# A graph network on one core: first layer's second product on full 128-row tiles, sender factors looked up with edges on partitions, one padding round of gathers left out

## What is computed

```python
h = relu(layernorm(x))
x = x + L0(h, src, dst)      # h scaled by out_degree**-0.5, summed over edges, times in_degree**-0.5
h = relu(layernorm(x))
# L1: encoders, then two steps over all edges and all nodes, then a decoder
n = ln(mlp(h));  e = ln(mlp(edge_attr))
for s in range(2):
    e = e + ln(mlp(concat(e, n[src], n[dst])))
    agg = segment_sum(e, dst)
    n = n + ln(mlp(concat(n, agg)))
out = x + mlp(n)
```

## Time and profile before

| | |
|---|---|
| median of 3 runs | 12197.94 us (12151.58 to 12213.49) |
| the profiled execution, its own time | 12234.22 us |
| its span, from first to last instruction | 12231.8 us |
| mean granted TensorE clock | 0.709 of full speed |
| busy: PE, PEld, DVE, ACT, POOL | 78%, 57%, 44%, 44%, 73% |

### The profile page before, as it was taken

The page is one execution under the profiler, slowest core; times in us unless marked ns, Lnnn a source line. Parts: engine busy times, 40 slices in busy tenths (PEclk is TensorE's granted clock), DMA queues, the critical chain, the costliest instruction groups (busy, mean ns, idle before and its releaser), DMA issues. The chain is left out here.

```text
span 12231.8 us, 206351 instructions
## 1 busy us (share of the span) xinstructions
PE 9512.5 (78%) x62224; PEld 6999.0 (57%) x62225; DVE 5436.7 (44%) x10951; ACT 5439.7 (44%) x8544; POOL 8971.4 (73%) x9433
## 2 busy tenths in 40 slices
PE   5889989999999967777777777776667677777776
PEld 4667777777788745555555555554444444444444
DVE  9744444455555534444444444443333333333333
ACT  0024444455555534444444444444444444444444
POOL 6757777777777367777777777776777777777776
PEclk8755555555555577777778777777777777777777
DMA  2222222222222233333333333342222222222222
GB/s 70 69 46 38 39 39 39 38 43 49 48 48 48 46 84 96 94 96 96 94 98 104 103 104 102 104 100 70 69 69 70 69 69 71 72 72 72 73 73 59
DMA packets 1311379, 869.26 MB, mean 71 GB/s; under 512 B 831441, under 2 KB 991442, under 8 KB 1309949
## 3 DMA queue, kind: packets, MB, share of 16 engines
q1 hardware_dynamic: 906914, 580.85, 16.9%
q0 software_dynamic: 301056, 231.81, 10.7%
q10 hardware_dynamic: 102736, 48.45, 1.5%
HBM read 629.10 MB, written 247.05 MB: 72 GB/s over the span
## 5 line engine op out<-in xcount | busy, mean ns | idle before, releaser
L1951 POOL DMA_INDIRECT edge_blk_g<-sender_part,idx_all x6272 | 5919.7, 944 | 2151.5 <-issue 1910.7
L148 POOL DMA_INDIRECT gather_ring<-sender_x,idx_all x2784 | 2631.8, 945 | 919.4 <-issue 843.2
L2007 PE MATMUL edge_blk_hps<-ident,edge_blk_g 128*128 128x128 f32 x6256 | 1224.6, 357 | 1971.1 <-DMA edge_blk_g<-sender_part,idx_all 1970.5
L2007 PEld LDWEIGHTS edge_blk_hps<-ident,edge_blk_g 128*128 128x128 f32 x6256 | 1048.5, 252 | 2723.7 <-DMA edge_blk_g<-sender_part,idx_all 2690.8
L2023 ACT ACT_TABLE_LOAD x1564 | 2006.6, 1283 | 59.3 <-ACTq L1113 31.5
L2095 DVE SCALAR_TENSOR_TENSOR agg<-edge_blk_aggps,vecs,agg 64x64 f32 x1564 | 441.9, 283 | 3073.7 <-PE edge_blk_aggps L1967 2919.0
L2037 ACT ACTIVATE edge_blk_h<-edge_blk_hps,vecs 128x512 f32<-128x512 f32 x782 | 537.2, 687 | 2794.7 <-PE edge_blk_hps L2007 2779.2
L2002 PE MATMUL edge_blk_hps<-edge_blk_oha,edge_blk_win 128*128 128x512 f32 x1564 | 1153.5, 828 | 27.8 <-DMA edge_blk_win<-receiver_part 27.8
L1990 PEld LDWEIGHTS edge_blk_yps<-w_edge_blk,edge_blk_h 64*128 64x128 f32 x12512 | 1011.0, 242 | 243.4 <-issue 243.4
L1990 PE MATMUL edge_blk_yps<-w_edge_blk,edge_blk_h 64*128 64x64 f32 x12512 | 1133.7, 336 | 0.0
L1656 ACT ACT_TABLE_LOAD x782 | 1003.3, 1283 | 274.1 <-PEq L91 260.3
(11 more groups left out here) (275 smaller groups left out, 12122.9 us busy)
## 6 DMA issues: line engine op xcount, KB each, us to landing
edge_blk_e<-edge_state SPq DMA_DIRECT2D x782, 256.0 KB
edge_blk_g<-sender_part,idx_all POOLq DMA_INDIRECT x6272
edge_state<-fl_e SPq DMA_DIRECT2D x391, 256.0 KB
edge_blk_dlb<-local_dst SPq DMA_DIRECT2D x1564, 64.0 KB
edge_state<-edge_blk_new SPq DMA_DIRECT2D x391, 256.0 KB
gather_ring<-sender_x,idx_all POOLq DMA_INDIRECT x2784
edge_blk_win<-receiver_part SPq DMA_DIRECT2D x1564, 16.0 KB
fl_attr<-attr_slots SPq DMA_DIRECT2D x391, 32.0 KB
```

What stands on the lines that cost most here:

```text
L148: pool.indirect_dma_start(out=gr[:, n % RING, j, :], out_offset=None, in_=table, in_offset=bass.IndirectOffsetOnAxis(ap=idx_all[:, 8 * n + ...
L1951: pool.indirect_dma_start(out=g[n % QUAD][:, i, 64 * c:64 * c + 64], out_offset=None, in_=ps_d, in_offset=bass.IndirectOffsetOnAxis(ap=idx ...
L2007: ins = nc.tensor.matmul(h_ps[n.half][:, P * i:P * i + P], g[n.b][:, i, :], ident[:, :], start=False, stop=i == TILES - 1)
```

## The change

- Lookup: the operands of `look` change places. The one-hot of 128 edges is now the stationary one, and the table's three parts of 128 columns stream past it: 24 matmuls a round in place of six of 512 columns. The result has edges on partitions. `pick` is then eight instructions of 128 columns that compare a row of numbers with each edge's low digit (`lo_e`, taken from `idx_all`), multiply, and write the sum out as well (`accum_out`). `total`, its column of ones, its PSUM banks, the spreading DMA of the low digits and the thirty dummy matmuls are gone.
- `EARLY` 44 to 40 and `AHEAD` 53 to 46.
- The float copy of each block's sender list moves from ACT to DVE.
- Setup: ACT's square root comes ahead of its wait for the copied lists.
- First layer: `second` is one bias matmul of 512 columns and four of 128 rows by 128 columns (the weights are block-diagonal), into one PSUM bank, the two banks taken by rounds in turn, so it waits for the norm of two rounds back. `encode` has weights of 128 rows, 64 of them zeros. The dummies of `stream` are gone.
- `every_round` issues rounds 0 to 390.

```diff
-EARLY = 44
-AHEAD = 53
+EARLY = 40
+AHEAD = 46
...
-    for n in range(first, FAST_ROUNDS):
+    for n in range(first, FAST_ROUNDS - 1):
         body(n)
...
+                    act.wait_ge(s_var, 1)
+                    nc.scalar.activation(rinv[:, :], red[:, :], ACT.Sqrt, bias=eps_c[:, 0:1], scale=1.0 / X_DIM).then_inc(s_dev, 1)
                     act.wait_ge(s_cp, 64)
...
-                    act.wait_ge(s_var, 1)
-                    nc.scalar.activation(rinv[:, :], red[:, :], ACT.Sqrt, bias=eps_c[:, 0:1], scale=1.0 / X_DIM).then_inc(s_dev, 1)
...
-                    nc.scalar.activation(srow_f[:, :], srow[:, :], ACT.Copy)
...
+                    if later(k):
+                        dve.wait_ge(tr_done, k)
+                    v.tensor_copy(srow_f[:, :], srow[:, :]).then_inc(srow_ok, 1)
...
                 def pick(r):
                     dve.wait_ge(z_ok, r + 1)
                     if r >= 2:
-                        dve.wait_ge(fac_ok, r - 1)
-                    v.scalar_tensor_tensor(picked[r % 2], lo_bc[r % 3][:, :], part_f[:, 0:1],
-                                           z_ps[r % 2][:, :, :].rearrange("p c e -> p (c e)"), ALU.is_equal, ALU.mult).then_inc(picked_ok, 1)
+                        dve.wait_ge(picked_ok, r - 1)
+                    for j in range(8):
+                        at = 8 * r + j
+                        ins = v.scalar_tensor_tensor(unsummed[:, r % 2, j, :], row_f[:, :], lo_e[:, at:at + 1],
+                                                     z_ps[r % 2][:, j // TILES, P * (j % TILES):P * (j % TILES) + P], ALU.is_equal, ALU.mult,
+                                                     accum_out=fac[:, at:at + 1])
+                    ins.then_inc(picked_ok, 1)
...
-                    for c in range(2):
+                    for j in range(8):
                         for i in range(3):
-                            ins = nc.tensor.matmul(z_ps[r % 2][:, c, :], r_parts[0:NHI, i, :], hi_hot[r % 2][0:NHI, CHUNK * c:CHUNK * c + CHUNK],
-                                                   start=i == 0, stop=i == 2)
+                            ins = nc.tensor.matmul(z_ps[r % 2][:, j // TILES, P * (j % TILES):P * (j % TILES) + P],
+                                                   hi_hot[r % 2][0:NHI, P * j:P * j + P], r_parts[0:NHI, i, :], start=i == 0, stop=i == 2)
...
-                for _ in range(30):
-                    nc.tensor.matmul(z_ps[1][:, 1, :], busy[:, 0:P], busy[:, :], start=True, stop=True)
                 pe.wait_ge(parts_ok, 1)
-                look(0)
                 for r in range(EARLY):
-                    if r + 1 < EARLY:
-                        look(r + 1)
-                    total(r)
+                    look(r)
...
-        attr_t = many(2, "attr_t", [64, P])
+        attr_t = many(2, "attr_t", [P, P])
...
-        y_ps = ctx.enter_context(nc.psum_tensor("fl_yps", [P, 2, 512], F32))
+        y_ps = [ps("yps0"), ps("yps1")]
...
-                    wait(pe, t_ok, n.back(1))
-                    for c in range(2):
-                        nc.tensor.matmul(y_ps[:, c, 0:TILES * D], one_bf[:, :], b1_parts[:, 0:TILES * D], start=True, stop=False)
+                    wait(pe, t_ok, n.back(2))
+                    y = y_ps[n.half]
+                    nc.tensor.matmul(y[:, :], one_bf[:, :], b1_parts[:, :], start=True, stop=False)
                     for i in range(TILES):
-                        for c in range(2):
-                            q = slice(64 * c, 64 * c + 64)
-                            ins = nc.tensor.matmul(y_ps[:, c, D * i:D * i + D], h[n.half][q, P * i:P * i + P], w_mid[q, q],
-                                                   start=False, stop=i == TILES - 1)
+                        ins = nc.tensor.matmul(y[:, P * i:P * i + P], h[n.half][:, P * i:P * i + P], w_mid[:, :],
+                                               start=False, stop=i == TILES - 1)
...
-                    if i is None and (n.b == QUAD - 1 if not isinstance(n.m, int) else n.n < 6):
-                        stream(8)
```

More of the change, by code:

```diff
@@ L138, in every_round @@
     with pool.If(sort > 0):
-        for n in range(FAST_ROUNDS, MAX_ROUNDS):
+        for n in range(FAST_ROUNDS - 1, MAX_ROUNDS - 1):
             body(n)
@@ L732, in edge_lists @@
         hi_bc = [sb(f"hi_bc{i}", [P, ROUND], BF16) for i in range(3)]
-        lo_bc = [sb(f"lo_bc{i}", [P, ROUND], BF16) for i in range(3)]
-        one_f = sb("one_f", [P, 1])
-        busy = sb("busy", [P, CHUNK], BF16)
+        lo_i, lo_e, fac = sb("lo_i", [P, EARLY * 8], I32), sb("lo_e", [P, EARLY * 8]), sb("fac", [P, EARLY * 8])
+        unsummed = sb("unsummed", [P, 2, 8, P], BF16)
         one_lo = [sb(f"one_lo{i}", [P, most_lo * P], BF16) for i in range(2)]
@@ L779, in rows @@
                     if later(k):
-                        for waited, value in ((rows_f, k), (digits, k)):
+                        for waited, value in ((rows_f, k), (srow_ok, k)):
                             sp.wait_ge(waited, value)
@@ L875, in _ @@
                 v.memset(zeros[:, :], 0.0).then_inc(zero_ok, 1)
-                v.memset(one_f[:, :], 1.0).then_inc(zero_ok, 1)
-                v.memset(busy[:, :], 1.0).then_inc(zero_ok, 1)
                 v.memset(deg[:, :], 0.0).then_inc(zero_ok, 1)
                 v.memset(zero_col[:, :], 0.0).then_inc(zero_ok, 1)
-                dve.wait_ge(zero_ok, 5)
+                dve.wait_ge(zero_ok, 3)
                 dve.wait_ge(base_in, 32)
@@ L974, in scale @@
                     rows = gr[:, first:last, :, :].rearrange("p r j c -> p (r j) c")
-                    v.tensor_tensor(rows, rows, fac_ps[k % 2][:, 0:8 * (last - first)].rearrange("p (r j) -> p r j", j=1).broadcast_to(
+                    v.tensor_tensor(rows, rows, fac[:, 8 * first:8 * last].rearrange("p (r j) -> p r j", j=1).broadcast_to(
                         [P, 8 * (last - first), X_DIM]), ALU.mult).then_inc(scaled, 1)
+                dve.wait_ge(lists_ok, LIST_BLOCKS)
+                v.tensor_scalar(lo_i[:, :], idx_all[:, 0:EARLY * 8], P - 1, None, ALU.bitwise_and).then_inc(lo_step, 1)
+                dve.wait_ge(lo_step, 1)
+                v.tensor_copy(lo_e[:, :], lo_i[:, :]).then_inc(lo_step, 1)
+                dve.wait_ge(lo_step, 2)
                 hot(0)
@@ L1613, in body @@
                         rest_of_weights(n)
-                def stream(k):
-                    for _ in range(k):
-                        nc.tensor.matmul(n_ps[:, :], one_bf[:, :], b1_parts[:, :], start=True, stop=True)
                 def rest_of_weights(n):
@@ L1635, in _ @@
                 pe.wait_ge(s_ld, weights_landed)
[L1636 removed]
+                nc.tensor.matmul(y_ps[0][:, 0:NVEC], mean_w[:, :], vecs[:, :], start=True, stop=True).then_inc(s_vm, 1)
                 pe.wait_ge(s_diag, 1)
                 k = VEC.index("edge_enc")
[L1639 removed]
+                nc.tensor.matmul(y_ps[1][:, 0:D], ones_d[:, :], diag[k][:, :], start=True, stop=True).then_inc(s_rows, 1)
                 pe.wait_ge(prepared, 1)
[L1641 removed]
                 last = rounds_and_nodes(pe, body, count_sb, 2)
@@ L1661, in scale @@
                     wait(act, y_ok, n)
-                    nc.scalar.activation(sq[:, :, :].rearrange("p (c i) d -> p c (i d)", c=2), y_all, ACT.Square).then_inc(sq_ok, 1)
+                    nc.scalar.activation(sq[:, :, :].rearrange("p k d -> p (k d)"), y_ps[n.half][:, :], ACT.Square).then_inc(sq_ok, 1)
                     wait(act, red_ok, n)
@@ L1827, in rest_of_weights @@
                         step(v.tensor_tensor(vecs[:, c:c + 1], vecs[:, c:c + 1], n_ps[:, m:m + 1], ALU.add))
+                for a in attr_t:
+                    step(v.memset(a[:, :], 0.0))
                 for b in range(QUAD):
@@ L1838, in _ @@
                 dve.wait_ge(s_vm, 1)
[L1839 removed]
+                step(v.tensor_copy(vmean[:, :], y_ps[0][:, 0:NVEC]))
                 centre_bias(["edge_enc"])
```

64 lines of the change are left out of this document (23 added, 41 removed).

## The result

| | before | after |
|---|---|---|
| median | 12203.60 us (4 runs, 12151.58 to 12213.49) | 11993.07 us (4 runs, 11992.40 to 11994.65) |
| profiled execution, its span | 12231.8 us | 11991.4 us |
| mean granted TensorE clock | 0.709 | 0.779 |

The ratio is 0.9836, with a 95% interval of 0.9808 to 0.9864. The runs of before are those of the table ahead and one more (12209.26); they spread over 0.5%, those of after over 0.02%.

A forecast was written before the change was run, and what follows sets the result against it. It took POOL's gathers to bound both edge steps and PE's loop the first layer. 12231.8 − 211 = 12021, with 2.4 around the span 12023, scaled by 0.3% to 11988 (chance 0.60); range 11935 to 12060.

The forecast's parts named there:

- The scaling: Whole time: profiled execution is 0.3% over the median of the runs, so the span sum of 12023 becomes 11988.
- Setup: Before the lists: ACT's root issued at once when the variance is ready, near 19.6 us; −4.4 us.
- Lists: Making of sender lists: float copies on DVE +4.5 us, fewer copies −1, low digits +0.8; all together 0, first look near 483.6.
- Lookup: Lookup rounds on DVE: eight picks of 0.36 us plus `hot` 0.48, 3.36 us a round (2.9 to 4.2), 40 rounds 134 us.
- POOL goes on at 628: End of the lookup: POOL resumes gathers at 628, not 738; its 46 rounds issued by 588, never the late one.
- First layer, POOL: First layer's gathers: 345 rounds at 9.99 us, 3448 us from 628 to 4076; smaller lead costs 60 us.
- First layer, PE: First layer's loop: 8.44 us a round, merge giving 0.1 to 0.15, through at 3937, before POOL's 4076; catches up near round 300.
- The rule against the merge: First layer's products: a weight load overlaps a running matmul only when row groups differ; halves had this, full tiles don't.
- padding round: End of edge steps: dropping it costed at nothing; rival that it was on the path, each step 10 us earlier, 11968, chance 0.05.
- Cold first layer: Rival, first layer: clock may stay at 0.5 without dummies and with other shapes, rounds of 8.86 us; 12006, chance 0.18.
- In series: Rival, lookup: hot, look and pick run one after the other, 6.2 us a round, 114 us of gain gone; 12102, chance 0.10.
- slower: Rival, first layer: full-row loads and streams don't overlap, 3.2 us more a round, 11.6; about 13090, chance 0.03.

## Why the prediction came out as it did

The forecast of 11988 lies 5 us below the median of 11993, and the mechanism (the first layer turns from PE's pace to POOL's) is the one that came. That it lies so near is luck, for two misses cancel in it: the sum gave a span of 12021, and 11991.4 came, while the scaling took 36 us off.

- **The scaling** of the profiled execution by 0.3%, 36 us, was a step that failed. Only kernels whose first layer ends with PE have such a spread: 0.35 to 0.95% in the groups of before, 0.37% with the lookup alone. Once POOL ends it, profiled execution and median agree within 0.03%. So the 36 us most likely lay in PE's first layer, which the change takes off the path, and nothing of them was left to scale; this is inferred from which kernels spread, as there is only one trace of before. The span's sum should have stood as it was, at 12023, and it would then have been 30 us over the median that came.
- **Setup:** −4.4 forecast. The first gather came 7.6 us earlier. I let ACT's table load stand behind the variance; with no wait ahead of it the load was done at 10.7. The variance came 1.6 us earlier too (16.1, not 17.7), and DVE's pause is 0.47 us.
- **Lists:** all together 0 forecast, first look near 483.6; `hot`, which comes just before it, starts at 475.74. The added copy on DVE cost nearly nothing: the lookup alone, without the setup's edit, has its first `hot` at 483.46, 0.7 later than before.
- **Lookup:** 3.36 us a round forecast (8 x 0.36 + 0.48). From the first pick at 479.13 to 591.7, less 5.8 us for three `scale`, 40 rounds take 107 us, 2.67 each. The picks are 0.27 apart, not 0.36: a record of 0.34 us starts 0.07 before the last one ends, which the two rows I drew the line through could not show, and the accumulator's read is hidden. It is two instructions, as the Trainium skill, "VectorE: DVE Perf Modes", section "Two Vector instructions with no wait between them", says, and the trace has 320 such reads; what they cost here is 0.014 us each at most.
- **POOL goes on at 628 forecast**, 598.21 came: 7.9 us from the earlier start, 26.6 from the shorter rounds, less 4.7, since the start came 8.16 us after POOL's own end and not 1.8 after DVE's. "Never the late one here" was wrong: POOL ended its 46 rounds at 590.05, with the lookup.
- **First layer, POOL:** 345 rounds, 3448 us forecast; from 598.21 to 4045.2 it took 3447. The next step came 45.4 us after that; 44.3 forecast.
- **First layer, PE:** 8.44 us a round and a catch-up near round 300 forecast; 6.9 us and round 160 came. The step that failed is that the clock stays. With the old shapes and no dummies the loop is 8.5 us, it catches up only after some 350 rounds, and the time is the same, so the miss changed nothing in the time. The prices of the pieces were right: 0.21 apart at the lower clock.
- **The rule against the merge**, of the Trainium skill, "TensorE: Matmul & The Clock Gate", Part 3, "The mechanism": at the lower clock the full pieces took 1.91 us for eight, the halves 1.97 for sixteen. So the pieces gave 0.06 us, and with the bias (0.40 us to the first piece, not 0.53) the merge gave 0.19 where 0.1 to 0.15 was forecast. What it gave beyond came from the clock, of which that section's rule says nothing. The prediction called 0.110 us a half piece and 0.214 a full one agreement with the rule. They are not: a half piece streams 64 columns and a full one 128, so both cost the same a column, and no price of a lost overlap shows in them.
- **Second bank, padding round, edge steps:** nothing forecast; 6.8 against 6.9 us a round without the bank, 1 us a step at most for the padding, 3951.5 us for the step.
- **The rivals.** Cold first layer: its condition holds in the kernel with the old shapes (clock 0.52 to 0.57), but its 12006 did not come (11993.87), since the round there is 8.5 us, which POOL hides, and with node work 8.8 and not 9.06 (91 transposes in 2600 to 3400). In series, no effect, and slower did not come: DVE was busy 95% of the lookup, and the full pieces came no more than 0.21 us apart. Nor did the steps end 10 us earlier without the padding round.

## What to carry to other kernels

When a stage goes from one engine's pace to another's, find that other engine's end first: here the dummies alone and the merge alone each brought the first layer to it (span 170 and 168 us less), the lookup alone gave 131, and all together 240. The 70 us beyond the dummies are all POOL's: its pause before the first layer falls from 71 to 8 us, and its first gather comes 7.6 earlier. New lookup and dropped dummies, with the old shapes, reach the same 11993.87. Do not scale a forecast by the spread of the kernel before, if the change takes away what spreads. Once an engine is the whole path, count its own rounds in every stage before believing that a wait elsewhere sets a start.

## What the runs showed of the hardware

- **The granted clock rose with the rows of the products, while PE was busy less.** In 1000 to 1400, the old shapes kept PE busy 367 of 400 us at 0.52, the new ones 264 of 400 at 0.91. Going from 64 to 128 rows in the encoder, with the new rows all zeros, raised it from 0.52 to 0.74 and, with the second product on 128 rows, from 0.56 to 0.91. Ones in one operand did the same. Dummies of 96 rows and 512 columns, eight in every fourth round, did not raise it (0.54 with, 0.53 without; 0.86 with, 0.91 without).
- **The same fp32 pieces cost nearly half at that clock:** 1.91 us for eight at the lower, 1.06 at the higher.
- **A gather is slower to issue while the lists are made.** POOL's group in the changed kernel in 240 to 340, and in 475 to 515:

```profile
L148 POOL DMA_INDIRECT gather_ring<-normed_x,idx_all x66 | 81.7, 1239 | 20.1 <-issue 20.1
...
L148 POOL DMA_INDIRECT gather_ring<-normed_x,idx_all x33 | 31.4, 951 | 10.1 <-issue 10.1
```

With its 0.30 us of issue one takes 1.54 us in the first stretch and 1.25 in the second, with the same table and ring. What differs is the other engines' work and the transfers for the lists. With POOL the whole path, that is the next place to look: some 280 gathers by 476 us at 0.29 us more each are 80 us, an estimate. What slows them was not tried.
- **A pause of 8.16 us** between POOL's last gather of the lookup and its first of the next Block came in every kernel with the new lead, also where DVE was done 4 us earlier; with the old lead it was 4.89. The cause was not sought.
